# A graph-attention layer whose source scores come as a 65th word of the gathered table row, in place of one-hot products

## The reference, cut to what matters

```python
h = x @ Wr                       # one 64x64 matrix for each of 8 relations
s = h @ a_src                    # the source score, one number per node and relation
d = h @ a_dst
e = leaky_relu(s[src] + d[dst])  # per edge, for the relation of the edge
m = segment_max(e, dst); w = exp(e - m[dst])
alpha = w / segment_sum(w, dst)[dst]
out += segment_sum(alpha[:, None] * h[src], dst)
```

## Time and profile before

| what | us |
|---|---|
| median of 3 runs | 5005.94 |
| the 3 runs | 5001.85 to 5008.78 |
| the profiled execution, first to last instruction (its span) | 7674.3 |
| span less median | 2668.4 |

### The profile page before, as it was taken

One profiled execution on the slowest core, in us unless ns is written; L12 is line 12 of the kernel. 1 busy time (PEld: TensorE's weight loads), 2 busy tenths in 40 slices (PEclk: granted clock), 3 DMA queues, 4 the chain that ended last, 5 costly groups with the idle time before them and its releaser, 6 DMA issues.

```text
span 7674.3 us, 62690 instructions
## 1 busy us (share of the span) xinstructions
PE 2780.9 (36%) x10695; PEld 1383.0 (18%) x10695; DVE 3909.1 (51%) x10509; ACT 1037.0 (14%) x2413; POOL 3533.6 (46%) x3645
## 2 busy tenths in 40 slices
PE   2116200156600000390003333333345556555695
PEld 1114100012300000280001111111122222222232
DVE  4127200499700000399765555555545666666995
ACT  0000000012100000280352111111120000000232
POOL 5650577300177777400003555555536566654463
PEclk5555555567755555695556666676667877777897
DMA  8100000046321111000342665565627777776593
GB/s 310 44 22 13 10 1 0 0 180 235 133 67 48 47 47 47 22 0 0 113 149 71 223 205 200 198 201 197 207 99 242 246 244 244 245 246 206 209 332 116
DMA packets 458408, 1039.68 MB, mean 135 GB/s; under 512 B 129581, under 2 KB 247829, under 8 KB 428140
## 3 DMA queue, kind: packets, MB, share of 16 engines
q1 hardware_dynamic: 167594, 579.38, 21.3%
q0 software_dynamic: 131968, 217.09, 10.3%
q10 hardware_dynamic: 158658, 241.42, 8.9%
HBM read 559.03 MB, written 476.15 MB: 135 GB/s over the span
## 4 chain that ended last, share of the span: by engine, by line
issue 28%; DVE 27%; another core or an unknown queue 22%; PE 9%; DVEq 9%; ACT 2%; ACTq 1%; DMA 1%; POOL 0%; SPq 0%; POOLq 0%
DVE arena L1786 6%; DVEq L110 3%; PE psum L1438 2%; DVE arena L1931 2%; DVE arena L2173 2%; DVE arena L1948 2%; DVEq L1786 1%; PE psum L1133 1%; DVE arena L2177 1%; ACT arena L969 1%; PE psum L1267 1%; PE psum L1255 1%; DVE arena L1575 1%; DVE psum L1851 1%
## 5 line engine op out<-in xcount | busy, mean ns | idle before, releaser
L715 POOL DMA_INDIRECT arena<-tab,ring x2352 | 2334.4, 993 | 1397.6 <-issue 1141.6
L1357 PE MATMUL psum<-arena,ident 128*128 128x512 f32 x1176 | 746.6, 722 | 1465.6 <-DVE arena L1786 1348.6
L1786 DVE SCALAR_TENSOR_TENSOR arena<-arena,ns 128x64 f32<-128x64 f32 (+2 forms) x2351 | 871.7, 371 | 612.0 <-issue 464.0
L757 POOL DMA_INDIRECT weights<-arena x784 | 774.1, 987 | 385.1 <-issue 331.6
L1931 DVE SCALAR_TENSOR_TENSOR arena<-iota_row,base,psum 128x200 f32<-128x200 f32 x784 | 278.1, 418 | 1082.8 <-remote 672.0
L1358 PE MATMUL psum<-arena,ident 128*128 128x512 f32 x1176 | 686.9, 669 | 0.0
L1321 PE MATMUL psum<-agg,arena 128*128 128x200 bf16 x2352 | 263.1, 267 | 1047.8 <-issue 943.4
L1357 PEld LDWEIGHTS psum<-arena,ident 128*128 128x128 f32 x1176 | 252.1, 229 | 1855.2 <-issue 1341.7
L704 POOL DMA_INDIRECT put<-arena,zidx x75 | 73.5, 979 | 745.3 <-DVE arena L1899 630.4
L1321 PEld LDWEIGHTS psum<-agg,arena 128*128 128x128 bf16 x2352 | 211.4, 104 | 1085.5 <-issue 991.1
L2275 DVE SCALAR_TENSOR_TENSOR arena<-psum,rowb 128x1024 f32<-128x1024 f32 x196 | 238.9, 1219 | 312.6 <-remote 297.0
(11 more groups left out here) (424 smaller groups left out, 4679.9 us busy)
## 6 DMA issues: line engine op xcount, KB each, us to landing
put<-zero SPq DMA_DIRECT2D x98, 1040.0 KB
arena<-put SPq DMA_DIRECT2D x98, 1040.0 KB
spill<-arena ACTq DMA_DIRECT2D x98, 1024.0 KB
arena<-spill SPq DMA_DIRECT2D x98, 1024.0 KB
state<-arena ACTq DMA_DIRECT2D x147, 512.0 KB
weights<-zero SPq DMA_DIRECT2D x32, 1600.0 KB
arena<-weights SPq DMA_DIRECT2D x32, 1600.0 KB, 7.3
put<-zero SPq DMA_DIRECT2D x14, 3584.0 KB
```

The lines of the kernel that those rows point to most:

```text
L715: pool.indirect_dma_start(out=rows[:, h, k, :], out_offset=None, in_=table[:, :], in_offset=bass.IndirectOffsetOnAxis(ap=ring[:, h, word + ...
L757: pool.indirect_dma_start(out=weights0[:, :], out_offset=bass.IndirectOffsetOnAxis(ap=words0[:, g, k:k + 1], axis=0), in_=words0f[:, g, K ...
L1357: pe.matmul(place, lhsT=ident[:, :], rhs=rows_of[0][:, s, columns, 0:width], start=True, stop=False)
L1786: beats.add(dve.scalar_tensor_tensor(out=rows[:, s, k, :], in0=before, scalar=mark(ns, g, k), in1=rows[:, s, k, :], op0=ALU.mult, op1=ALU. ...
```

## The change

Each row of `tab1` becomes 65 words (`W1`). The 65th is the source score of that node and relation. The gather brings it along, the store to DRAM leaves it out, and ACT copies it from the ring to `score[:, 0, :]`, one copy per group. The one-hot path of step 3 is gone from PE, ACT and DVE, with the preparation that it had on DVE. DVE no longer waits for source scores before the scans of step 4 but ahead of line 2019, and there for all 98 groups. POOL has one more wait before it refills a slot.

```diff
-        tab0, tab1 = dram("tab0", [NP, D]), dram("tab1", [NP * R, D])
+        tab0, tab1 = dram("tab0", [NP, D]), dram("tab1", [NP * R, W1])
...
-                sp.dma_start(group_rows(spill1, g), g1[:, s, :, :]).then_inc(kept[s], 16)
+                sp.dma_start(group_rows(spill1, g), g1[:, s, :, 0:D]).then_inc(kept[s], 16)
...
-                ready((ring_in[s], uses[0] * 16 + 16), *(((kept[s], uses[0] * 16),) if late(g, 4) else ()))
+                ready((ring_in[s], uses[0] * 16 + 16), *(((kept[s], uses[0] * 16), (picked1, g - 3)) if late(g, 4) else ()))
...
-            def pick1(u, h):
-                act.wait_ge(spread1, u + 1)
-                act.activation(bank(h), bank(h), ACT.Square, bias=own_row[:, 0:1]).then_inc(apart1, 1)
-                act.wait_ge(apart1, u + 1)
-                if late(u, 2):
-                    act.wait_ge(sifting, u - 1)
-                act.activation(picks[:, h, :, :].rearrange("p k n -> p (k n)"), bank(h), ACT.Relu, bias=1.0, scale=-1.0).then_inc(hot1, 1)
-            units(act, pick1)
+            def pick1(g, s, uses):
+                act.wait_ge(got[s], uses[0] * 16 * K + 16 * K)
+                act.activation(score[:, 0, bass.ds(g * K, K)], g1[:, s, :, D:W1].rearrange("p k c -> p (k c)"), ACT.Copy).then_inc(picked1, 1)
+            quads(act, pick1)
...
-                    message = act.activation(y1[:, s, k, :], rows[:, s, k, :], ACT.Copy, scale=alpha1[:, bass.ds(g * K, K)][:, k:k + 1])
+                    message = act.activation(y1[:, s, k, :], rows[:, s, k, 0:D], ACT.Copy, scale=alpha1[:, bass.ds(g * K, K)][:, k:k + 1])
...
-            def spread1_of(u, h):
-            def sift1(u, h):
-            units(pe, source_scores)
-            sift1(UNITS - 1, (UNITS - 1) % 2)
...
-                        beats1.add(dve.tensor_copy(s_all[:, at, :], scores[:, :, 0:R]))
+                        beats1.add(dve.tensor_copy(tb1[:, :, :, D:W1].rearrange("p j r c -> p j (r c)"), scores[:, :, 0:R]))
...
-                    dve.tensor_copy(tb1[:, lo:hi, :, :].rearrange("p j r c -> p (j r) c"), product(lo * R * D, (hi - lo) * R * D, D)).then_inc(used, 1)
+                    dve.tensor_copy(tb1[:, lo:hi, :, 0:D].rearrange("p j r c -> p (j r) c"), product(lo * R * D, (hi - lo) * R * D, D)).then_inc(used, 1)
...
-            def select1(u, h):
-            units(dve, scores1)
-            select1(UNITS - 1, (UNITS - 1) % 2)
-            dve.wait_ge(picked1, UNITS)
...
+            dve.wait_ge(picked1, NG)
             step(dve.tensor_tensor(ev, s_src, dsel, ALU.add))
```

More of the change, by code:

```diff
@@ L64 @@
 ORDER = sorted(range(NT + T // PB), key=lambda t: (t + 1) / NT if t < NT else (t - NT + 1) / (T // PB))
-UNITS = T // 4
+W1 = D + 1
 W2 = HID + D
@@ L142, in windows @@
         body(w)
[L145 to L151, removed]
 def gnn_program(nc, x, src, dst, etype, adj_v, deg_v, w0, b0, deg_coeff, coeff_param, scale_param,
@@ L310, in gnn_program @@
         total0 = agg[:, :, :].rearrange("p i c -> p (i c)")
-        g1, ds = quad(25200, D), area(12600, T, 2 * R)
+        g1, ds = quad(25200, W1), area(12600, T, 2 * R)
         alpha1 = score[:, 0, :]
@@ L315, in gnn_program @@
         mixed0 = area(4000, NT, D)
-        tb1 = area(0, NB, R * D).rearrange("p j (r c) -> p j r c", c=D)
+        tb1 = area(0, NB, R * W1).rearrange("p j (r c) -> p j r c", c=W1)
         dn1 = area(3000, NT, 2 * R)
@@ L319, in gnn_program @@
         gc1, y1 = quad(0, D), quad(2200, D)
[L321 to L328, removed]
         cg = area(0, NT, D)
@@ L393, in gnn_program @@
         made1, filled1, weights_set = sem("made1"), sem("filled1"), sem("weights_set")
-        split1, spread1, hot1, sifting, picked1 = (sem(n) for n in ("split1", "spread1", "hot1", "sifting", "picked1"))
-        apart1 = sem("apart1")
+        picked1 = sem("picked1")
         filled2, summed2, work2, gate2, made2, scan2 = (sem(n) for n in ("filled2", "summed2", "work2", "gate2", "made2", "scan2"))
@@ L1302, in _ @@
             pe.wait_ge(taken, 2 * NBATCH)
-            pe.wait_ge(split1, 1)
-            def spread1_of(u, h):
[L1307 to L1312, removed]
-            def sift1(u, h):
[L1316 to L1329, removed]
-            units(pe, source_scores)
-            sift1(UNITS - 1, (UNITS - 1) % 2)
             carry(0, tails[:, :], R)
```

## The result

The change makes the kernel slower: 5571.01 us median (5569.33 to 5575.78, 4 runs) against 5005.5 us, a ratio of 1.1132, 95% interval 1.1116 to 1.1148, or +566 us. I had forecast 5466 us, with 5200 to 5600 as range.

The account below looks back on a forecast made before the run. Layer 1's gather by POOL was taken to hide the score work in the runs; late scores move its end from 939 to 823 + 576 = 1399 us, so 5006 + 460 = 5466 us, range 5200 to 5600.

Parts of the forecast that it names:

- The mechanism: Layer 1: source scores come with the last gather, at 823 us and not 300, delaying everything from line 2019; +460 us.
- the pitch of the gather: Time x per indirect DMA in the runs: taken as 1.05 us, from 0.95 to 1.25; 784 of them end at 823 us.
- my own sum: Layer 1 from the first gather: 823 + 576 = 1399 us after the change, against 939 before; +460 us.
- The upper bound: x = 1.25 us; from 1.18 on the layer 1 difference stays at +561 us; with 34 and 41 us added, up to 5600.
- the check against the time of the runs: All layers: without the profile's waits, savings at x = 1.05 of 2357 to 2690 us hold the 2668 us gap; 1.25 gives too little.
- The attribution to the recording: Waits behind PE instructions during the gather come from trace records let through at about one per indirect DMA, only when profiled.
- the changed kernel's span near 7340 us: Sign in the changed kernel's profile: span some 283 + 51 us shorter, 7340, while the time is some 460 us longer.
- Rival 1: Layer 1: the waits are in the runs too, so the change takes away 331 us, giving 4675 us; chance 0.13.
- Rival 2: Layer 1 score units slowed in part, 600 us in all: change costs 175 us, 5180 us, range 5020 to 5350; chance 0.10.
- The parts costed at nothing: Layer 1's gather: ACT's copies (at most 34 us), POOL's extra wait (at worst 34), longer rows and smaller store pieces (41 if 5% slower).

## Why the prediction was right, and what of it was not

**The mechanism held.** On a chip like that of the result, scores and scans are ready 347 us after the first gather (351 forecast), and the changed kernel makes line 2019 wait for the end of the gather. The wait for 70 groups shows the price of such lateness alone: +272 us, with everything else of the kernel before in place. The changed kernel is as late again: 280 us of further lateness at line 2019, and 283 us of further span. The kernels without scores show, on chips of the second kind, that the changed kernel and the wait for 98 groups come to the same layer 1, 1650 us. That lateness is all of the 566 us on the result's chip is put together from 272 and 283, since no run with the wait for 98 groups is from a chip of the first kind.

**The term that was mis-sized is the pitch of the gather**, x = 1.05 us. It is 1.25, which was my upper bound, in the changed kernel and in the run with a wait for 70 groups alike: the gather takes 978 us, not 823. With 1.25 my own sum gives 980 + 576 - 995 = +561 us, 5 us from the measured 566, where the point forecast of +460 was 106 short. The upper bound carried the range: the measured time lies 29 us under its end. The pitch of 1.25 stood in the rows; I talked myself out of it by the check against the time of the runs. That check was wrong in layer 0. It speaks of 450 us of sums that can start beside the scatter, but its totals let only 330 of them do so, and no reason is given for the rest. In the run with a wait for 70 groups the first gather of layer 1 starts at 1155.5 us against 2098.5 in the profile before, 943 us sooner, where my sum had 800 at the most for 1.25. The other two were near: the gathers of layers 2 and 3 take 995 and 1009 us where they took 1395 and 1258, savings of 399 and 249 for the 464 and 260 in the sum.

**The attribution to the recording was wrong as put.** Two traces of the first kind record PE's matmuls beside indirect DMAs without being held back: that of the changed kernel in layer 0, that of the wait for 70 groups in the gather of layer 1 too. So recording alone doesn't bring the waits. And on three chips all runs of the kernel before are long. The check by the time had said that the waits of the earlier trace rows could not be in the runs of 5005 us, and this was so; the cause that I named for them was wrong. I also expected the changed kernel's span near 7340 us; it was 5567.4 on the chip of the result and 7326.7 on one of the second kind, so that number was right for the wrong reason.

**Rival 1** is no rival but the other kind of chip: -318 us measured, -331 worked out. The page that I cited, "Runtime: NRT & Kernel Launch" of the Trainium skill (preamble/postamble breakdown), has a profile's total some 6.2 us above the reported time. The spans here, from first to last instruction, lie 1.9 and 1.8 us under the time of their own runs: 5567.4 and 5569.33 us, 7612.8 and 7614.58. So the nearness agrees, the sign doesn't. I had read the gap of 2668 us as a failure of that rule. A chip of the second kind for the trace and one of the first for the runs explains it: 7674.3 us is within 0.4% of the 7645 us of such a chip. The record doesn't name the chip, so this is not shown. **Rival 2** (units slowed in part) did not show: 1.50 us a unit, 294 us in all.

**The parts costed at nothing.** ACT's 98 copies take 0.21 us each and wait for DMA alone. On the first kind of chip POOL's pitch is 1.25 us with the new wait and without it. Rows of 65 words alone: ratio 1.0008, on the second kind. From the last gather's start to line 2019: 2.9 us, 3 forecast.

**What stays open.** What tells the chips apart, whether it is the chip or the session, and what holds small instructions to the pace of the indirect DMAs. That each instruction sends something that has to be let through is my guess; nothing in the traces names it. Whether the waits of the second kind would be there with no recording isn't shown either. Neither kernel is the better one everywhere: on the first kind of chip it is the kernel before, whose scores are ready before the gather ends, on the second the changed one.

## What to carry to other kernels

Fetching a value with data that is being gathered anyway saves work, but the value is then complete only when the gather is. If another path delivers it earlier beside the gather, and a chain of 571 us hangs on it, the saved 300 us of hidden work are worth nothing and the lateness is worth everything. And where a profile's span is not near the time of the runs, first ask whether the two come from the same machine: the trace shown here looks like those of chips on which the same change has the other sign.

## What the runs showed of the hardware that was not expected

The same program took 5005 to 5010 us on one kind of chip and 7608 to 7645 on the other (medians). On the second, while POOL issues indirect DMAs, an engine that waits for PE starts late, by 1.24 to 1.46 us for each PE instruction before it (45 us a unit with 32, 21 to 24 with 16). ACT's message instructions, each 0.35 us long, start mostly 1.40 us apart. Long DVE instructions are not affected: in the kernel with a wait for 98 groups and no scores, step 4's scans and selections took 51.2 us beside the gather (2118.17 to 2169.38), as they did in the trace before with no gather beside them. The last wait ends some 18 us after the last indirect DMA starts. On the first kind 81 indirect DMAs and 1073 matmuls share 100 us with no loss to either.
